# The next step's up weights asked for by ScalarE, and the adapter input split earlier in the step, in a two-layer conditional block on one core

## What is computed

```python
def adapter(x, lang):                      # W1: 512x128, W2: 128x512, one of 10
    h = relu(x @ W1[lang] + b1[lang])
    y = x + h @ W2[lang] + b2[lang]
    return layernorm(y) * gamma[lang] + beta[lang]
x = x + adapter(x, lang)
def mlp(x, e):                             # W1: 512x2048, shared W2: 2048x384, We: 2048x128
    h = gelu(x @ W1 + b1)                  # exact gelu
    return concat([h @ W2 + b2, h @ We[e] + be[e]])
x = x + mlp(x, expert)
```

## Time and profile before

| | us |
|---|---|
| median of 3 runs | 1652.06 (1651.17 to 1652.21) |
| the profiled execution | 1646.32 |
| its span, first to last instruction | 1644.5 |

### The profile page before, as it was taken

How to read it: one execution, slowest core, us unless ns; L and a number is a source line. 1 busy time by engine, 2 the same in 40 slices (tenths; PEclk the granted TensorE clock), 3 DMA queues, 4 the chain that set the end, 5 groups by cost and what they waited for, 6 DMA issues and landing times.

```text
span 1644.5 us, 19032 instructions
## 1 busy us (share of the span) xinstructions
PE 1477.5 (90%) x6400; PEld 1202.0 (73%) x6400; DVE 976.8 (59%) x1620; ACT 514.9 (31%) x822; POOL 689.9 (42%) x672
## 2 busy tenths in 40 slices
PE   3457869999899989999899998999899998999999
PEld 2346657878687767877778786887678777888887
DVE  4855466565755566646566657555665566664444
ACT  2242333423233222423234332342224232242222
POOL 3746351383416633453324825155433533343111
PEclk8579989999999999999999999999999999999999
DMA  7332644645347344464335553363544653344333
GB/s 236 116 109 93 204 160 154 233 170 195 128 141 256 127 146 160 168 212 175 133 137 192 185 195 128 141 230 119 180 160 152 220 180 105 123 153 167 141 141 103
DMA packets 127761, 265.91 MB, mean 162 GB/s; under 512 B 11696, under 2 KB 83632, under 8 KB 119472
## 3 DMA queue, kind: packets, MB, share of 16 engines
q1 hardware_dynamic: 127664, 264.69, 46.3%
HBM read 226.90 MB, written 37.75 MB: 161 GB/s over the span
## 4 chain that ended last, share of the span: by engine, by line
PE 68%; DVE 9%; issue 7%; POOL 6%; DMA 4%; ACT 3%; SPq 2%; DVEq 0%; ACTq 0%; POOLq 0%
PE down L201 12%; PE down L203 12%; PE down L202 12%; PE up_b L201 4%; PE up_b L203 4%; PE up_b L202 4%; PE up_a L201 3%; PE up_a L203 3%; PE up_a L202 3%; PE up_c L201 2%; PE up_c L203 2%; PE up_c L202 2%; DMA w_raw<-m_we 2%; DVE x L625 2%; DVE xTs L589 2%
## 5 line engine op out<-in xcount | busy, mean ns | idle before, releaser
L564 DVE TENSOR_TENSOR g<-g_raw,g 128x512 fp32r<-128x512 f32 x256 | 216.8, 854 | 349.9 <-ACT g L416 349.8
L201 PE MATMUL down<-w,g 128*128 128x512 f32 x1024 | 402.3, 393 | 4.0 <-issue 3.8
L202 PE MATMUL down<-w,g 128*128 128x512 f32 x1024 | 399.4, 390 | 0.0
L203 PE MATMUL down<-w,g 128*128 128x512 f32 x1024 | 399.1, 390 | 0.0
L769 POOL TENSOR_TENSOR w<-w_raw,ones 128x256 fp32r<-128x256 f32 x128 | 83.1, 649 | 655.2 <-DMA w_raw<-m_we 655.1
L201 PEld LDWEIGHTS down<-w,g 128*128 128x128 f32 x1024 | 193.7, 189 | 44.9 <-issue 4.4
L202 PEld LDWEIGHTS down<-w,g 128*128 128x128 f32 x1024 | 193.4, 189 | 40.1
L203 PEld LDWEIGHTS down<-w,g 128*128 128x128 f32 x1024 | 192.8, 188 | 40.6
L201 PE MATMUL up_b<-bo,w 128*128 128x512 f32 x384 | 157.4, 410 | 67.4 <-DVE u L544 59.1
L416 ACT CAST g<-g_raw 128x512 fp32r<-128x512 f32 x256 | 159.2, 622 | 8.1
L414 ACT ACTIVATE g_raw<-u,m_b_sb 128x512 f32<-128x512 f32 x64 | 46.4, 724 | 357.5 <-PE down L203 316.8
(11 more groups left out here) (154 smaller groups left out, 2453.6 us busy)
## 6 DMA issues: line engine op xcount, KB each, us to landing
w<-w_kept SPq DMA_DIRECT2D x56, 1792.0 KB, 7.7
w<-w_kept SPq DMA_DIRECT2D x56, 768.0 KB, 4.9
w_raw<-m_we SPq DMA_DIRECT2D x128, 128.0 KB, 4.5
out<-resid SPq DMA_DIRECT2D x64, 256.0 KB, 4.8
xs<-x SPq DMA_DIRECT2D x60, 256.0 KB, 5.5
xTs_raw<-xT SPq DMA_DIRECT2D x56, 256.0 KB, 3.3
w_kept<-w SPq DMA_DIRECT2D x8, 1792.0 KB, 7.8
aw_raw<-a_w SPq DMA_DIRECT2D x30, 256.0 KB, 7.3
```

Source lines behind the costliest of these rows:

```text
L201: eng.matmul(bank, a_hi, b_hi, start=opens, stop=False, skip_group_check=True)
L202: eng.matmul(bank, a_hi, b_lo, start=False, stop=False, skip_group_check=True)
L203: return eng.matmul(bank, a_lo, b_hi, start=False, stop=closes, skip_group_check=True)
L564: eng.tensor_tensor(g[:, b, k % 2, h, LO, :], g_raw[:, b, k % 2, h, LO, :], raw(g[:, b, k % 2, h, HI, :]), ALU.subtract).then_inc(dve_glo, 1)
```

## The change

Three things are done. The requests for the streamed up weights (`load_w1`) leave SyncE's list and stand in ScalarE's, between the cast of C21 of the step before and the copy `s1`; they go out on ScalarE's own queue. The high and low parts of the adapter input are made in the first half of each step: on ScalarE before gelu of C11 (in steps 1 to 3 it was behind), on VectorE before the down sums and `u2` (it was behind `u2` in step 0 and behind C12 in steps 1 to 3). And the request for the second batch's relu bias (`load_b1(eng, m, 1, ...)`) moves from step 4 to step 3.

```diff
@@ act_step
+        if i is not first and k < GROUPS - 1:
+            load_w1(eng, i, k + 1)
+        if m and k == GROUPS - 1:
+            load_w1(eng, m, 0)
         act_first_sum(eng, i, k)
...
         if m:
-            if k == 0:
-                act_xT_hi(eng, m, 0, 0)
-                act_xT_hi(eng, m, 0, 1)
             if k in (2, 4):
                 act_relu(eng, m, k // 2 - 1)
+            if k in ADAPTER_UP:
+                b, c = ADAPTER_UP[k]
+                act_xT_hi(eng, m, b, c)
+                act_xT_hi(eng, m, b, c + 1)
...
         act_g(eng, i, k, C11)
         if m:
-            if k in (1, 2, 3):
-                b, c = ADAPTER_UP[k]
-                act_xT_hi(eng, m, b, c)
-                act_xT_hi(eng, m, b, c + 1)
@@ dve_step
             if k in (2, 4):
                 dve_h0_lo(eng, m, k // 2 - 1)
+            if k in ADAPTER_UP:
+                b, c = ADAPTER_UP[k]
+                dve_xT_lo(eng, m, b, c)
+                dve_xT_lo(eng, m, b, c + 1)
             if k - 1 in ADAPTER_DOWN:
                 b, t = ADAPTER_DOWN[k - 1]
                 dve_finish(eng, m, b, t)
...
         dve_sum_u2(eng, i, k)
-        if m and k == 0:
-            dve_xT_lo(eng, m, 0, 0)
-            dve_xT_lo(eng, m, 0, 1)
         dve_g_lo(eng, i, k, C11)
         dve_sum_c12(eng, i, k)
-        if m and k in (1, 2, 3):
-            b, c = ADAPTER_UP[k]
-            dve_xT_lo(eng, m, b, c)
-            dve_xT_lo(eng, m, b, c + 1)
@@ sp_pair
-            elif k < GROUPS - 1:
-                load_w1(eng, i, k + 1)
-            if m and k == GROUPS - 1:
-                load_w1(eng, m, 0)
...
                 if k == 3:
+                    load_b1(eng, m, 1, language_b)
                     load_biases(eng, m, 1, language_b)
...
                 if k == 4:
                     load_aw(eng, m, 1, 1, language_b)
-                    load_b1(eng, m, 1, language_b)
                     load_gamma(eng, m, 1, language_b)
```

## The result

| | before | after |
|---|---|---|
| median us | 1652.13 (4 runs, 1651.17 to 1652.47) | 1611.76 (4 runs, 1609.57 to 1613.39) |
| the profiled execution | 1646.32 | 1612.66 |
| its span | 1644.5 | 1610.9 |
| mean granted clock | 0.958 | 0.966 |

The ratio is 0.9756, with a 95% interval of 0.9739 to 0.9773: 40.4 us faster. The forecast was 57 us and 1595; the measured time is 0.2 us inside the slow end of the range (1612), which is luck more than reading. The two profiled executions differ by 33.7 us only. That of before lay 5.8 under its median and that of after 0.9 over it, so 6.7 us of the 40.4 are in no trace.

What follows compares the result with a forecast made beforehand. TensorE, 90% busy, was taken as the bound, with only its waits and the clock able to give time back. 29.6 + 12 + 5.4 + 10 + 0 = 57 us off the 1652 median gave 1595 us, range 1580 to 1612.

Steps and rivals of the forecast that it cites:

- The bias in step 3: Step 4, pairs 1 to 6: an earlier bias request ends the relu's wait, gaining 29.6 us plus 12 of clock.
- Pair 0: In pair 0, the earlier bias gains 4 us and the earlier split 1.4, together 5.4 us.
- Steps 1 and 2: Pairs 1 to 6: low-part waits go, TensorE's adapter product moves up to just behind GpSimd's chain, gaining 10 us.
- Step 0: Low parts now ahead of the down sums; TensorE does not wait there, so the cost is 0.
- Rival B: VectorE and GpSimd slow each other in step 3 (9 us) and step 4 (4 more): 1608 us, chance 0.17.
- Step 3: Low-part waits of 2.4 us go, a 2.4 loss from late `u2` cancels them: 0, from +2.4 to -9.
- The up weights from ScalarE: Moving the up-weight requests to ScalarE's queue delays nothing TensorE needs and gains nothing: costed at 0.
- Rival D: Up weights, asked for later, land too late and stall TensorE at some 55 loads: 1705 us, chance 0.04.
- Rival A: GpSimd is not the limit in steps 1 and 2; all 23.5 us of waits return: 1582 us, chance 0.14.
- The period: Sign to check: the period of pairs 1 to 6 falls from 193 us to about 184, else the forecast is wrong.

Runs made afterwards that it cites:

- experiment 1: The kernel before with only the request for the second batch's relu bias moved from step 4 to step 3: 1599.53 us, ratio 0.969.
- experiment 2: The kernel before with only the up-weight requests moved to ScalarE's queue, bias and split left as they were: 1605.88 us, ratio 0.9734.
- experiment 4: The changed kernel with the adapter input split put back as before, leaving the bias and queue moves: 1600.30 us, ratio 0.9706 to before.
- experiment 3: The kernel before with only the adapter input split moved to the first half of each step: 1661.81 us, ratio 1.0063.
- experiment 5: The changed kernel with GpSimd splitting step 2's adapter weights ahead of the residual and bias sums: 1567.96 us, ratio 0.9482 to before.
- experiment 7: experiment 4 with the GpSimd edit of experiment 5, so adapter weights first but without the split: 1594.82 us, ratio 0.9661 to before.
- experiment 6: experiment 5 with the two low parts of step 0 put back behind `u2` on VectorE: 1561.39 us, ratio 0.9442 to before.
- Experiment 8: experiment 6 with GpSimd's 1/sqrt moved ahead of weight sums and experts' weights in steps 3 to 6: 1534.83 us, ratio 0.9296 to before.

## Why the prediction was right and wrong

**The bias in step 3: right.** Step 4 and its clock were to give 29.6 + 12 = 41.6 us; they gave 44.1, and in experiment 1, by itself, 44.8. The argument that asked plus 7.0 us hits the relu's start to 0.1 us named a releaser that the profile did not, and experiments 1 and 2 took the wait away by two ways. Of the 0.3 us that was to stay in each step, 0.22 did as a mean (21.98 against the 21.76 of pair 4), but not for the reason I gave. I had costed the request on ScalarE at 0.4, and it cost nothing there: it starts at 963.97, within the cast that ends at 964.53, and `s1` follows at 964.43. In pair 4 the relu starts 2.68 us behind the start of the step both in experiment 1, without the request, and in experiment 4, with it. What did grow is VectorE's part: in that step the two instructions that end the layer norm take 1.41 us in experiment 1 and 3.48 in experiment 4.

**Pair 0: right.** 5.4 forecast, 4 for the bias and 1.4 for the split. The change measured 4.4, the bias alone (experiment 1) 5.0, the split alone (experiment 3) 1.6.

**Steps 1 and 2: wrong, and the term that failed.** The step reads: "It can move to about 0.1 us behind GpSimd and no further". The mechanism was right, and TensorE did start 0.05 us behind GpSimd. The sum made of it was not. A gain of 10 us was forecast, a loss of 7.0 measured, 17 us apart. The failed term is "10 us", which took the length of GpSimd's chain as fixed and the clock behind the new wait as nearly free. Worked out from the timelines of all six pairs, the 17 fall apart in two:

| pair | 1 | 2 | 3 | 4 | 5 | 6 | sum of differences |
|---|---|---|---|---|---|---|---|
| end of GpSimd's chain, us behind the start of step 1, before | 38.92 | 38.03 | 38.06 | 38.89 | 37.88 | 38.12 | |
| the same, after | 39.91 | 39.40 | 39.41 | 39.73 | 39.47 | 39.47 | +7.5 |
| from the adapter product to the end of step 2, before | 9.64 | 9.64 | 9.62 | 9.64 | 9.64 | 9.61 | |
| the same, after | 11.25 | 11.27 | 11.24 | 11.26 | 11.27 | 11.28 | +9.8 |

- The clock, 9.8 of the 17. I had set "a short fall of the clock behind the new waits of about 2 us" against a gain in the experts' transfer, and counted neither. But TensorE now comes to that product without any wait in step 1, so the slack that had been spread over steps 1 and 2 stands in one piece. The wait is 3.9 to 4.2 us, not 2, and the clock falls behind each of the six. The prediction had the material for it: the six waits of step 4, of 5 us, had cost 2 each, and even in the kernel before two of the four waits of 1.8 to 2.0 us in step 1 were followed by a lower clock. These are windows of 6 us behind the ones of pairs 3 and 5, where it fell, and 2 and 6, where it did not (columns as above):

```profile
727.21:733.21 6.00, 5.50 (x17) 0.72 0.30 90
1112.27:1118.27 6.00, 5.27 (x16) 0.72 0.33 111
533.91:539.91 6.00, 5.27 (x22) 1.00 0.40 139
1305.32:1311.32 6.00, 5.27 (x22) 1.00 0.40 132
```

- GpSimd's chain, 7.5 of the 17. It starts as early in the step as before (4.1 to 4.4 us behind the start of step 1 in both kernels), so the experts' weights landed no sooner for standing ahead of the up weights. But it takes 35.3 to 35.6 us where it took 33.8 to 34.8. In pair 4 the growth is 0.72 us (34.76 to 35.48), in pairs 2, 3, 5 and 6 it is 1.4 to 1.5. The chain is as long in experiment 3 (35.3 to 35.6), so the split did it. The low parts now lie beside GpSimd's work, and each slows the other. GpSimd's residuals, the same 64 instructions, show it; first in before, then in after (busy us, mean ns of one):

```profile
L762 POOL TENSOR_TENSOR resid<-x,m_bias 128x512 f32<-128x512 f32 x64 | 84.7, 1359 | 0.0
```

```profile
L760 POOL TENSOR_TENSOR resid<-x,m_bias 128x512 f32<-128x512 f32 x64 | 93.2, 1487 | 0.0
```

TensorE starts 0.05 us behind the chain and not 0.1, which gives 0.3 back, and so the two make up the 17.

**Step 0: wrong.** "TensorE does not wait there, and product 7 comes about 1 us after `u2` could be ready. 0." It cost 5.8 us in the change, and undoing it gave 6.6 by the medians, 4.9 by the lengths of step 0. I had the slack, 1 us, and two low parts of 688 ns against it, and should have taken the long form of up to 1772, since GpSimd is at work there. Rival B had this mechanism, but put it in step 3 and step 4. In step 3 it cost 0.5 us in all, not 9, and in step 4 at most the 0.2 us a pair named above. B's time, 1608, came nearest of all those written down, partly by luck: its cause acted in other steps, in step 0 and in GpSimd's chain, and the 9.8 us of the clock are not in it.

**Step 3: right.** A loss of 2.4 against a gain of 2.4 was forecast, a loss of 0.5 measured. The sign that went with it did not hold: the wait for `u2` there is 0.64 to 1.07 us, not under 0.5 (rival B: 1.5).

**The up weights from ScalarE: right that nothing is lost, but not for its reason.** Rival D did not come: no wait of TensorE for `w` is in the list. "I cost the queue at nothing" holds for the whole change, where the bias was moved as well (experiment 4 against 1). It would have been wrong by 46 us for the queue alone. I wrote that none of the requests behind it is waited for by TensorE "apart from the bias", and did not follow that exception up.

**Rival A: wrong.** It gave steps 1 and 2 all their waits back. Its condition, GpSimd not being the limit, was made true in experiment 5, and there steps 1 and 2 do come to 44.88 together, 4.8 under before in each pair.

**The period** was to come down from 193 to about 184; the step lengths of after add up to 188.0. The sum of the parts: forecast 41.6 + 5.4 + 10 + 0 = 57; measured 44.1 + 4.4 - 7.0 - 5.8 - 0.5 = 35.2, less 1.5 in step 5 and ahead of pair 0, is 33.7; and 6.7 that no trace shows.

Two things stay open. The 6.7 us are mostly the difference between one profiled execution of before and its median (5.8); the executions of before went from 1644.0 to 1656.69, and no trace of a slower one exists. And step 1 is 0.4 to 1.3 us longer in experiments 1, 2, 4 and 7 than in before. Most of it is that the first wait of step 1 was only 1.0 us in pairs 1 and 4 of before, where it is 1.4 to 2.0 in these kernels, and that the clock fell in step 1 in 2 of the six pairs of before and in 3, 5, 2 and 3 of them here. Why it falls behind one such wait and not behind the next is not shown.

## What to carry to other kernels

When a wait is removed, ask of the next late thing not only when it comes but how long a wait stands in front of it in one piece: here waits of up to 2 us, which cost clock only at times, joined into one of 4, which cost clock every time. Before a request is called free, read what stands behind it in its engine's list and what in it waits; here a transfer of 0.5 KB behind a large one whose request waits was worth 46 us. And two engines that each hold the same product must be changed together: here either edit alone gave nothing or a loss, both together 33 us.

## What the runs showed of the hardware that I had not expected

**VectorE beside GpSimd.** At their new places the 56 low parts went from a median of 688 ns to 1225:

```profile
L590 DVE TENSOR_TENSOR xTs<-xTs_raw,xTs x56: 675/1225/1780, 80.4 to 1320.3; 128x512 fp32r<-128x512 f32 x56
```

With the split put back and nothing else (experiment 4) they are at 683; with the split alone (experiment 3) they are at 1271:

```profile
L593 DVE TENSOR_TENSOR xTs<-xTs_raw,xTs x56: 674/683/1784, 80.2 to 1312.8; 128x512 fp32r<-128x512 f32 x56
```

GpSimd pays too. Its busy time is 685.4 to 690.2 us in the kernels without the split (before and experiments 1, 2, 4, 7) and 702.9 to 709.3 in those with it (after and experiments 3, 5, 6), for the same instructions. (Experiment 8 is at 724.6, but its 1/sqrt is recorded at 976 ns as a mean, and that of experiment 6 at 783.) The Trainium skill says (SBUF — State Buffer, "Who interferes with whom") that such a VectorE instruction and a GpSimd instruction that reads SBUF block each other. The numbers above agree in kind. By the rule every such meeting costs, and what the row of before could not tell is how many there would be.

**The clock behind a wait.** Waits of 4.0 to 4.2 us in front of the adapter product were followed by 0.72 to 0.76 of the clock over 6 to 7 us. In the kernel before a wait of 1.80 us at the same place was followed by full clock, and I had taken waits of "about 2 us" for nearly harmless. They are not safe either: over before and experiments 1, 2, 4 and 7 a first wait of 1.7 to 2.0 us in step 1 stands 27 times, and 15 of them were followed by a lower clock. The waits of 3.9 to 4.2 us in step 2, in after and experiment 3, were so 12 times out of 12.

**A request on ScalarE** takes 0.33 us, as on SyncE, and overlapped the cast before it. In step 4 of pair 4 neither the copy nor the relu behind it started later in the step with it (experiment 4: 2.20 and 2.68 us) than without it (experiment 1: 2.21 and 2.68).
